# Casting a kernel's weights to bf16: through on-chip buffers and GpSimd, or by five DRAM-to-DRAM transfers

## The reference

```python
xn = layernorm(x)
# branch 1: a recurrence over the 2048 positions, then a layer norm
xB = xn @ B.T                                  # 1024 -> 128
state = tanh(state @ A.T + xB[t])              # for t in 0..2047
y  = (states @ C.T + D * xn) + xn
a  = (y - mean(y)) * rsqrt(var(y) + eps) * gamma + beta
# branch 2: a feed-forward net with ternary weights, tlin(x, w, s) = (x @ w.T) * s
h = silu(tlin(xn, w1, s1)) * tlin(xn, w2, s2)  # 1024 -> 4096
h = gelu(tlin(h, h1, h1s))                     # 4096 -> 4096
h = gelu(tlin(h, h2, h2s))                     # 4096 -> 4096
f = tlin(h, w3, w3s)                           # 4096 -> 1024
out = x + a + f
```

## Time and profile before

| What | us |
|---|---|
| the two timed runs | 7170.92 and 7479.51 |
| their median | 7325.21 |
| the profiled execution, its time | 7176.55 |
| the profiled execution, its span (slowest core, core 6) | 7175.0 |
| spans of the 8 cores | 7133.5 to 7175.0 |
| TensorE busy | 5305.3 (74% of the span) |
| VectorE busy | 1469.3 (20%) |
| ScalarE busy | 666.6 (9%) |
| GpSimd busy | 430.9 (6%) |
| TensorE weight loads (beside matmuls) | 2437.7 (34%) |

### The profile page before, as it was taken

One profiled execution on the slowest core, in us unless ns is written; L12 is line 12 of the kernel. 1 busy time (PEld: TensorE's weight loads), 2 busy tenths in 40 slices (PEclk: granted clock), 3 DMA queues, 4 the chain that ended last, 5 costly groups with the idle time before them and its releaser, 6 DMA issues.

```text
span 7175.0 us, 66520 instructions; the slowest of 8 cores (7133.5 to 7175.0 us)
## 1 busy us (share of the span) xinstructions
PE 5305.3 (74%) x24252; PEld 2437.7 (34%) x24252; DVE 1469.3 (20%) x2720; ACT 666.6 (9%) x1334; POOL 430.9 (6%) x340
## 2 busy tenths in 40 slices
PE   0421111499959995999599959995999599958996
PEld 0310000144424442444244423442344234423442
DVE  3421127620042004200330033003300330024002
ACT  0012210010001000100010001000100010001000
POOL 0033333100000000000000000000000000000000
PEclk9999999999979997999799979997999799979998
DMA  3289999544424442444244424442344344433442
GB/s 115 89 289 312 304 301 302 184 142 152 153 98 143 153 150 100 138 153 153 100 141 153 153 101 140 153 153 100 135 153 153 106 135 153 150 115 124 153 153 103
DMA packets 264147, 1121.30 MB, mean 156 GB/s; under 512 B 26900, under 2 KB 28181, under 8 KB 190104
## 3 DMA queue, kind: packets, MB, share of 16 engines
q1 hardware_dynamic: 236184, 1016.38, 41.6%
q0 software_dynamic: 23040, 83.90, 3.6%
q10 hardware_dynamic: 4608, 16.78, 0.8%
HBM read 1007.90 MB, written 109.05 MB: 156 GB/s over the span
## 4 chain that ended last, share of the span: by engine, by line
PE 67%; DVE 6%; DMA 5%; issue 2%; ACT 1%; SPq 0%; POOL 0%; DVEq 0%; POOLq 0%; ACTq 0%
PE pE L669 49%; PE pA L608 6%; PE pB L613 5%; PE pG L697 3%; PE pH L697 3%; DMA xrb<-x 3%; DMA l1ring<-w2b 2%; PE pA L551 1%; DVE xnbt L560 1%; DVE t2b L737 1%; DVE t1b L740 1%; DVE t1b L754 1%; DVE t1b L748 1%; DVE t2b L751 1%; ACT thbuf L621 0%
## 5 line engine op out<-in xcount | busy, mean ns | idle before, releaser
L669 PE MATMUL pE<-hbuf,hring 128*128 128x512 bf16 x8192 | 1779.3, 380 | 29.6 <-DVE hbuf L639 28.8
L669 PE MATMUL pE<-g1buf,hring 128*128 128x512 bf16 x8192 | 1770.0, 379 | 9.7 <-ACT g1buf L676 7.4
L669 PEld LDWEIGHTS pE<-hbuf,hring 128*128 128x128 bf16 x8192 | 803.1, 98 | 1005.8 <-issue 47.9
L669 PEld LDWEIGHTS pE<-g1buf,hring 128*128 128x128 bf16 x8192 | 800.5, 98 | 979.3 <-issue 16.1
L705 DVE TENSOR_SCALAR ffn_fm<-pG,w3spk_s 128x512 f32<-128x512 f32 x32 | 24.0, 751 | 3774.9 <-PE pG L697 3774.9
L608 PE MATMUL pA<-xnbt,l1ring 128*128 128x512 bf16 x2048 | 500.4, 388 | 100.8 <-DMA l1ring<-w2b 47.8
L613 PE MATMUL pB<-xnbt,l1ring 128*128 128x512 bf16 x2048 | 486.9, 381 | 0.0
L456 PE MATMUL pE<-states,atb 128*128 128x8 bf16 x560 | 97.7, 174 | 523.0 <-ACT states L463 523.0
L370 POOL CAST cout<-cinr 128x2048 bf16<-128x2048 f32 x176 | 341.4, 1941 | 603.5 <-DMA cinr<-h2t 243.6
L770 POOL DMA_DIRECT2D out<-out_sb x32 | 17.2, 536 | 5659.6 <-DVE out_sb L763 5659.6
L621 ACT ACTIVATE thbuf<-pA,s1h 128x512 f32<-128x512 f32 x256 | 175.9, 687 | 1902.3 <-PE pB L613 1899.5
(11 more groups left out here) (76 smaller groups left out, 2036.9 us busy)
## 6 DMA issues: line engine op xcount, KB each, us to landing
hring<-h1b SPq DMA_DIRECT2D x256, 1024.0 KB, 4.9
hring<-h2b SPq DMA_DIRECT2D x256, 1024.0 KB, 4.8
xrb<-x POOLq DMA_DIRECT2D x128, 512.0 KB, 4.3
cinr<-h1t SPq DMA_DIRECT2D x64, 1024.0 KB, 17.9
cinr<-h2t SPq DMA_DIRECT2D x64, 1024.0 KB, 19.7
l1ring<-w1b SPq DMA_DIRECT2D x256, 256.0 KB, 2.7
l1ring<-w2b SPq DMA_DIRECT2D x256, 256.0 KB, 2.9
hring<-w3b SPq DMA_DIRECT2D x64, 1024.0 KB, 4.8
```

What stands on the lines that cost most here:

```text
L669: op("tensor", lambda e, p=pe_, s=hs, kk=k, r=rsrc: e.matmul(p[:, 0:512], hslot(s)[:, kk * 128:(kk + 1) * 128], r[:, kk * 512:(kk + 1) * 512],
```

## The change

`emit_cast`, its units and its two buffers go. In their place POOL issues five transfers, one for each weight, straight from the f32 tensor in DRAM to the bf16 tensor in DRAM; the transfer converts. Each has a semaphore of its own, which SP's list waits for ahead of the first load of that weight in stage two (and which stands in the list of all semaphores that every engine waits for there). h1, h2 and w3 are laid out on the host in the order of their bf16 copies, so that source and target agree row by row.

```diff
-    h1t_d = nc.dram_tensor("h1t", [32, 4, 128, 1024], F32, kind="ExternalInput").ap()
+    h1t_d = nc.dram_tensor("h1t", [32, 128, 4096], F32, kind="ExternalInput").ap()
...
-        cinr = sb1("cinr", [128, 4 * 2048], F32)
-        cout = sb1("cout", [128, 4 * 2048], BF16)
...
-                    L4N[v] = dop("sync", lambda e, s=cast_units[v][0], d=cv2: e.dma_start(d, s),
-                                 clsems[sl])
...
-                cn = op("gpsimd", lambda e, sl=slot: e.tensor_copy(
-                    cout[:, sl * 2048:(sl + 1) * 2048],
-                    cinr[:, sl * 2048:(sl + 1) * 2048]), cv)
-                wait("sync", cv, cn)
...
-                S2N[u] = dop("sync", lambda e, d=cast_units[u][1], s=co2: e.dma_start(d, s),
-                             cssems[u % 4])
+        CSEM = {"w1": cl, "w2": clB, "h1": clC, "h2": clD, "w3": cv}
+        for nm_, s_, d_ in (("w1", w1t_d, w1b_d), ("w2", w2t_d, w2b_d),
+                            ("h1", h1t_d, h1b_d), ("h2", h2t_d, h2b_d),
+                            ("w3", w3t_d, w3b_d)):
+            op("gpsimd", lambda e, ss=s_, dd=d_: e.dma_start(dd, ss), CSEM[nm_], 16)
...
-            if n % 32 == 31:
-                emit_cast(cast_per)
...
-                    for s_, v_ in zip(cssems, csn(CS_W12_U - 1)):
-                        wait("sync", s_, v_)
+                    wait("sync", cl, 16)
+                    wait("sync", clB, 16)
...
-                    for s_, v_ in zip(cssems, csn(NCU - 1)):
-                        wait("sync", s_, v_)
+                    wait("sync", cv, 16)
```

More of the change, by code:

```diff
@@ L40, in _build @@
     w2t_d = nc.dram_tensor("w2t", [32, 128, 1024], F32, kind="ExternalInput").ap()
-    h1t_d = nc.dram_tensor("h1t", [32, 4, 128, 1024], F32, kind="ExternalInput").ap()
-    h2t_d = nc.dram_tensor("h2t", [32, 4, 128, 1024], F32, kind="ExternalInput").ap()
-    w3t_d = nc.dram_tensor("w3t", [8, 4, 128, 1024], F32, kind="ExternalInput").ap()
+    h1t_d = nc.dram_tensor("h1t", [32, 128, 4096], F32, kind="ExternalInput").ap()
+    h2t_d = nc.dram_tensor("h2t", [32, 128, 4096], F32, kind="ExternalInput").ap()
+    w3t_d = nc.dram_tensor("w3t", [8, 128, 4096], F32, kind="ExternalInput").ap()
     s1_d = nc.dram_tensor("s1pk", [128, 32], F32, kind="ExternalInput").ap()
@@ L312, in _build @@
             gset("pB0", (xb, xb.n))
[L314 to L363, removed]
-                    L4N[v] = dop("sync", lambda e, s=cast_units[v][0], d=cv2: e.dma_start(d, s),
-                                 clsems[sl])
[L366 to L369, removed]
-                cn = op("gpsimd", lambda e, sl=slot: e.tensor_copy(
-                    cout[:, sl * 2048:(sl + 1) * 2048],
-                    cinr[:, sl * 2048:(sl + 1) * 2048]), cv)
-                wait("sync", cv, cn)
-                co2 = cout[:, slot * 2048:(slot + 1) * 2048]
-                if cast_units[u][1].ap is not None and len(cast_units[u][1].ap) == 3:
-                    co2 = co2.rearrange("p (m c) -> p m c", c=1024)
-                S2N[u] = dop("sync", lambda e, d=cast_units[u][1], s=co2: e.dma_start(d, s),
-                             cssems[u % 4])
@@ L446, in _build @@
         wait("scalar", xb, 32)
-        p2_batch = 0
-        cast_per = 20
         for n in range(NBURN + 512):
@@ L471, in _build @@
             emit_p2(j)
-        emit_cast(NCU)
         gset("pE", (ac, ac.n))
@@ L654, in _build @@
                     if tj == 0 and m == 0:
-                        for s_, v_ in zip(cssems, csn((CS_H1_U if lay == 0 else CS_H2_U) - 1)):
-                            wait("sync", s_, v_)
+                        wait("sync", clC if lay == 0 else clD, 16)
                     gwait("sync", ("hr", hs))
@@ L798, in _tile_hh @@
     v = wt.reshape(I // 1024, 8, 128, nm, 128)
-    return np.ascontiguousarray(v.transpose(3, 0, 2, 1, 4).reshape(nm, I // 1024, 128, 8 * 128))
+    return np.ascontiguousarray(v.transpose(3, 2, 0, 1, 4).reshape(nm, 128, I))
 def _prep_inputs(inputs):
```

## The result

| What | us |
|---|---|
| the changed kernel, its undisturbed runs | 7245.3 to 7257.6 |
| the kernel before, its undisturbed runs beside them | 7165.5 to 7170.9 |
| ratio, with its 95% interval | 1.0116 [1.0096, 1.0136] |
| median over all 13 runs of the changed kernel | 7849.5 |
| median over the 10 runs of the kernel before taken with them | 7307.0 |

The change made the kernel slower by 1.2%, some 83 us. In many runs of both kernels the cores of one die, or of both, have a lower granted clock and take longer (in the profiled execution those of die 1), so the two medians can't be set beside each other, and the ratio is of the undisturbed runs.

The account below looks back on a forecast made before the run. Stage one's end decides, set by casting at the transfers' pace and by VectorE's tail. Casts land at 1217 us, 27 units (173 us) follow, ending at 1390, 52 late: 7176.6 + 52 = 7229 us; 8-in-10 range 7060 to 7640.

Parts of the forecast that it names:

- 34 us as summed: VectorE's tail in stage one: three instructions, slowed by POOL's casts, would shorten over 32 units, 34 us in all.
- D: Length of the five DRAM-to-DRAM casts, taken as 835 us at 331 GB/s of total traffic; bounds 511 and 1222 us.
- the end of the tail: Stage one's last statistics unit on VectorE: 5 units by 1217 us, 27 x 6.42 = 173 us after, ending at 1390 us.
- 8 x 4.7 = 38 us: One x load in the tail: its 8 rows per engine each wait for a 64 KB cast row of 4.7 us.
- The bound of 42 us: Tail's x load at the likeliest case's slow end: 42 us each with casts of 917 us, giving 7301 us.
- 382 + 835 = 1217 us: Landing of the five casts in stage one: start at 382 us behind the x load, then 835 us of transfer.
- Stage two was said to be untouched: From the first l1ring load on, the change does not touch the second stage, kept at 5833 us.
- Casting out of the way: Rival on the casts: they take near 511 us and land before the scan is over; 7070 us, chance 0.13.
- both ends paid: Rival on the five transfers: engines pay for reading, then writing, 151 GB/s of source, landing at 1604 us; 7582 us, chance 0.25.
- Engines in each other's way: Rival on the casts: 16 engines read in step at power-of-two distances, 117 GB/s, landing at 1959 us; 7920 us, chance 0.12.

Follow-up runs that it names:

- the probe: Eight DRAM-to-DRAM transfers, one after another, ahead of the changed kernel's own work; f32 to bf16 took 76.8 us, f32 to f32 100.9, bf16 to bf16 50.2.
- twoq: The changed kernel with the tail's x loads for odd units on SP's queue, so two in flight; 7241 to 7266 us, ratio 1.0112 [1.0034, 1.0190].
- late4k: The changed kernel with casts in 4 KB rows and those of h2 and w3 issued in stage two; two undisturbed runs, 7355 and 7397 us.

## Why the prediction was right and wrong

**What held.** The mechanism held step by step: the transfers go by the sum of the bytes read and written, each x load waits for long rows, and VectorE has most of its units still to do when the casts land. A 64 KB row was put at 4.7 us and took 4.53 to 4.70. VectorE's three instructions fell to 0.81, 1.23 and 1.23 us, 34 us as summed. The middle of two rates that D rested on, 331 GB/s, is close to what GpSimd's three kinds of transfer show in the probe, 328 to 334, but that was luck: no row had such a transfer, the middle was only a choice between 302 and 361, and in the same probe a copy in 4 KB rows has 313 GB/s and SP's copy 353.

**The step that failed** is the end of the tail, "1390 us", in two terms of its sum that were both too small. One is the x load's price, "8 x 4.7 = 38 us". It was 45 to 50. The sum counted the 8 rows of data and left out the ninth packet on each engine, which the page of the kernel before already had (4608 packets for 32 loads), and the part of a load that is no wait for a row, 9.5 us by the three row lengths. VectorE's waits for x thus came to 187 us where some 160 were forecast. The bound of 42 us, called the long end, was no bound. The other is the landing, "382 + 835 = 1217 us". It was 1229: D was 849 us. The sum let the casts have the engines to themselves, but the x loads took 5.6% of the engines' time (1030 to 1200 us), which over the 208 us of the tail that the casts shared makes 12 us, by that estimate most of the 14 missing. With two loads in flight (twoq) the casts took 866 us.

Put into the prediction's own sum, with fractions of a unit kept, the true landing adds 11 us to the last unit's end, 50 us a load adds 8, and 6.33 us a unit in place of 6.42 takes 3 off: (1230 - 1022) / 50 = 4.2 units are done by the landing, and 1230 + 27.8 x 6.33 = 1406 us. Measured was 1407.

**The comparison.** The forecast was 7229 us against a profiled execution of 7176.6, a loss of 52 us; measured were 7250 against 7167 us in the mean of the undisturbed runs, a loss of 83, and the interval of the ratio is clear of 1. Held against the median of 7325 us that stands at the head, 7229 reads as a gain, and the change gave none. The last unit's end was taken from the slowest core, which ended stage one at 1341.7 us; the other cores ended it at 1317 us and up, and all eight lost, 80 us in the mean. The slowest core's first l1ring load went from 1342 to 1414 us, 72 us later, of which the forecast had 52 and the two terms above give 16 more. Stage two was said to be untouched, and the undisturbed runs bear that out within a few us.

**The rivals.** Casting out of the way (D near 511 us) and both ends paid (1222 us) are both excluded by D = 849. The second had the right idea, since reading and writing do add up; what was off is that they add up to some 330 GB/s in all, where 151 GB/s of source would be 227. Engines in each other's way: h1, with 64 rows of 64 KB for an engine if the engines take consecutive rows, landed at 378.9 + 465.1 = 844.0 us and w2 ahead of it at 378.4 + 157.6 = 536.0 us, so its 67.1 MB took 308 us, 218 GB/s of source, as fast as w1 in the probe. The Trainium skill's fall to 103 GB/s (DMA: Bandwidth & Descriptors, Latency and other measured facts) doesn't show here. GpSimd's transfers stopped at 334 GB/s, and SP's copy of the same f32 rows, with all eight cores at it, reached 353. So the 334 are not the limit of the memory; what holds GpSimd's transfers below SP's, no run tells. The 358 GB/s a core that the Trainium skill gives (HBM Reference, Specifications) lie 1.4% above SP's copy. Of the Trainium skill's rule that an engine drains a packet of many descriptors before it turns (DMA: Bandwidth & Descriptors, Queues, rings and completion order), the trace bears out the turns between queues; but an x load took nine of them, one for each of its nine packets on an engine, so in this case a row was a packet.

## What to carry to other kernels

Between 4 and 64 KB a transfer's row length cost the casts some 2% at most and a plain f32 copy 7%, but it set how long everybody else's small loads took: their packets on an engine times the time of one long row, and some us more. Before a bulk transfer is put beside a latency chain, load what the chain needs ahead of it, or give the chain deeper buffers; here that turned a loss of 1.2% into a gain of 1%. Then give the old kernel the same buffers before the gain is put down to the change: with 12 slots each, the old casting was the faster one, by some 40 us as far as one undisturbed run shows. Taking the casts off POOL freed 34 us of VectorE's time, and the x loads behind long rows cost it 113.

## What was not expected of the hardware

The conversion from f32 to bf16 inside a DRAM-to-DRAM transfer costs next to nothing: 328 GB/s of bytes read and written, against 332 and 334 for transfers without it. The same f32 copy was faster from SP's queue than from GpSimd's on every core, 92 to 99 us against 100 to 104. Two loads on two queues take the time of one (53 us against 50) while a third queue's long rows fill the engines. And waiting for weights costs TensorE twice: 172 us of waits for l1ring in late4k came with a granted clock of 0.77 over 402 us, and stage two grew by 286 us.
